# Two gather turns moved into the experts' program, batch 1's gathers moved up, and the last batch's steps rearranged

## The reference

```
layer 0:  q = layernorm(x);  x += tanh(g) * causal_attention(q, ctx, ctx)        16 heads of 32
          w, sel = top 8 of 32 experts of softmax(layernorm(x) @ gate_w)
          x += tanh(g') * sum over the 8 of  w * down(silu(gate(row)) * up(row))
layer 1:  q = rms_norm(layernorm(x) @ wq + bq); k = rms_norm(ctx @ wk + bk); v = ctx @ wv + bv
          x += tanh(g) * (softmax(q k^T / sqrt(32)) v @ wo + bo)
          out = x + tanh(g') * (layernorm(x) @ ternary(weight) + bias)
```

## Time and profile before

| what | us |
|---|---|
| median of 3 runs | 1456.93 (1450.17 to 1460.65) |
| the profiled execution | 1449.55 |
| its span | 1447.8 |
| PE busy in the span | 1290.1 (89%) |
| layer 0, up to its barrier | about 297 |
| experts, up to their barrier | 922.0 |
| layer 1, first scores to last step's end | about 968 to 1409 |

### The profile page before, as it was taken

One profiled execution on the slowest core, in us unless ns is written; L12 is line 12 of the kernel. 1 busy time (PEld: TensorE's weight loads), 2 busy tenths in 40 slices (PEclk: granted clock), 3 DMA queues, 4 the chain that ended last, 5 costly groups with the idle time before them and its releaser, 6 DMA issues. The chain is left out here.

```text
span 1447.8 us, 39176 instructions
## 1 busy us (share of the span) xinstructions
PE 1290.1 (89%) x11501; PEld 836.5 (58%) x11502; DVE 940.0 (65%) x2347; ACT 897.2 (62%) x1845; POOL 519.5 (36%) x537
## 2 busy tenths in 40 slices
PE   3999999559999999999999999756899999999984
PEld 3777777425556656665556666333565656656652
DVE  4699897655566655656555633164777888888863
ACT  4777776325566666666566666425667777777661
POOL 2036564664335333321000000655544555552000
PEclk9999999779999999999999999978999999999997
DMA  3036445499888676766766544856646646653000
GB/s 104 31 130 224 181 171 184 173 311 324 290 309 282 235 234 226 244 213 215 233 229 210 193 146 145 167 89 88 102 69 108 106 71 117 103 72 75 16 8 23
DMA packets 96136, 233.49 MB, mean 161 GB/s; under 512 B 11808, under 2 KB 11808, under 8 KB 91424
## 3 DMA queue, kind: packets, MB, share of 16 engines
q0 software_dynamic: 33712, 113.79, 31.5%
q1 hardware_dynamic: 62320, 118.34, 24.6%
HBM read 140.84 MB, written 91.24 MB: 160 GB/s over the span
## 5 line engine op out<-in xcount | busy, mean ns | idle before, releaser
L1614 PE MATMUL bank<-wh,xT 128*128 x1280 | 340.1, 328 | 6.3 <-DVE hp L1729 5.4
L709 POOL DMA_INDIRECT xs<-y_tiles,slot_ix x120 | 191.2, 1593 | 219.9 <-DMA y_tiles<-ysb 99.9
L1614 PE MATMUL bank<-wl,xT 128*128 x640 | 209.4, 327 | 0.0
L1719 DVE SCALAR_TENSOR_TENSOR hv<-bank,sg 128x192 f32<-128x192 f32 x160 | 57.0, 356 | 220.1 <-ACT sg L1673 174.6
L1688 ACT ACTIVATE ysb<-bank,xg 128x512 f32<-128x512 f32 x160 | 110.0, 687 | 117.5 <-PE bank L1638 117.5
L1614 PEld LDWEIGHTS bank<-wh,xT 128*128 128x128 f16 x1280 | 125.6, 98 | 83.6 <-issue 13.4
L1667 ACT ACTIVATE xT<-bank 128x1024 f16<-128x1024 f16 x160 | 162.7, 1017 | 15.3 <-PE bank L1602 15.3
L1638 PE MATMUL bank<-wh,hT 128*128 x480 | 155.8, 379 | 0.8 <-issue 0.5
L1849 PE MATMUL bank<-w_hi,halfT 128*128 128x512 f16 x384 | 127.1, 393 | 23.5 <-DVE accb L1966 22.1
L334 ACT ACTIVATE l_probs<-bank,l_bias 128x256 f32<-128x256 f32 x256 | 118.9, 473 | 39.0 <-DVE l_bias L368 38.6
L1508 POOL DMA_DIRECT2D raw<-in_experts_dram x30 | 16.8, 560 | 333.2 <-DVE wl L1745 325.4
(11 more groups left out here) (282 smaller groups left out, 3060.4 us busy)
## 6 DMA issues: line engine op xcount, KB each, us to landing
xg<-x_slots SPq DMA_DIRECT2D x160, 272.0 KB, 2.8
y_tiles<-ysb SPq DMA_DIRECT2D x160, 256.0 KB, 2.7
raw<-in_experts_dram POOLq DMA_DIRECT2D x30, 1280.0 KB, 7.3
x_slots<-blank SPq DMA_DIRECT2D x33, 272.0 KB, 4.0
xs<-in_x_dram SPq DMA_DIRECT2D x8, 512.0 KB, 6.4
cbuf<-in_ctx_dram SPq DMA_DIRECT2D x8, 512.0 KB, 4.4
stage<-in_mats_dram POOLq DMA_DIRECT2D x4, 1024.0 KB, 6.4
room<-in_ctx_dram SPq DMA_DIRECT2D x8, 512.0 KB, 5.7
```

The lines of the kernel that those rows point to most:

```text
L709: return nc.gpsimd.indirect_dma_start(to, None, self.y_tiles[0 : (MT + 1 - k) * P, :], ix, compute_op=ALU.add)
L1614: last = nc.tensor.matmul(bGU[t.place % 2][:, 0:GU], xT[:, t.place % 2, xo + c * P : xo + (c + 1) * P], wp[:, bass.ds(w, 1), c * GU : (c + ...
```

## The change

It has four parts. `LAST_ADDS` falls from 4 to 2: six turns of batch 0 in the experts' list, two in layer 1's. In `BEGIN1`, DVE does `xc` before `P2` and `xn`, `sx` before `P3`, ACT does `sx` before `k0`, `k1`, and POOL issues three gathers of batch 1 before `P1`. For the last batch, a table `LAST1` takes the place of `SIDE1`: batch 6's post part is placed earlier in its steps, and `a0`, `b0`, `c0`, `d0` of batch 7 itself (words with `=`) in steps 11 to 15. The ten sends of batch 6 that follow `pw` lose their waits.

```
-LAST_ADDS = 4
+LAST_ADDS = 2
 BEGIN1 = dict(
-    act=["sc", "T0", "T1", "P0", "P1", "k0", "k1", "sx", "T2", "T3", "P4", "P5", "k2", "k3"],
+    act=["sc", "T0", "T1", "P0", "P1", "sx", "k0", "k1", "T2", "T3", "P4", "P5", "k2", "k3"],
-    dve=["sc", "P0", "P1", "P2", "P3", "xc", "xn", "sx", "k0", "k1", "P4", "S0", "S1", "P5", ...
+    dve=["sc", "P0", "P1", "xc", "P2", "xn", "sx", "P3", "k0", "k1", "P4", "S0", "S1", "P5", ...
+LAST1 = dict(
+    pe={0: ["a0"], 1: ["a1"], 2: ["<c0"], 3: ["c1"], 4: ["<d0"], 5: ["<d1"], 8: ["<g0", "g1"], 9: ["h0"], 10: ["h1"], 11: ["=a0"],
+        13: ["<=c0"], 14: ["=d0"]},
+    act={1: ["b0", "b1"], 2: ["c0"], 3: ["c1"], 7: ["f0", "f1"], 8: ["g0"], 9: ["g1"], 12: ["=b0"], 13: ["=c0"]},
+    pool={5: ["d1"]},
+    dve={0: ["a0", "a1"], 1: ["b0"], 2: ["<b1"], 4: ["d0"], 5: ["d1"], 6: ["e"], 7: ["f0", "f1"], 10: ["h0"], 11: ["h1"],
+         12: ["<=a0", "=b0"], 15: ["=d0"]})
-def side1(table, b, step, early, do_prep, do_post):
+def side1(eng, b, step, early, do_prep, do_post):
+    table = LAST1[eng] if b.n == B - 1 else SIDE1[eng]
...
+        if piece.startswith("="):
+            do_post(b, piece[1:])
+        elif piece in ORDER_PREP1:
...
 (layer 0, POOL's end)
-            for n in (1, 2):
-                pool.wait_ge(xe_norm, QT * (B - 1) + n)
-                send_next()
-            for n in (1, 2):
-                pool.wait_ge(post_copied, 2 * (B - 1) + n)
-                send_next()
-            for n in (11, 12, 13, 14, 16, 18):
-                pool.wait_ge(dve_post, marks + n)
+            while sends[0] < SENDS * (B - 1):
                 send_next()
...
+        LAST_USES = ["a0", "c0", "d0", "a1", "c1", "d1", "g0", "g1", "h0", "h1"]
...
 (dve_post_, piece a)
+                if is_last(b):
+                    dve.wait_ge(at.probs_made, STEPS * b.n + STEPS // 2 * (t + 1))
+                    chain.link(v.reciprocal(rsum[:, t, :], at.sums[:, b.par, t, :]))
+                elif t == 0:
                     dve.wait_ge(at.probs_made, STEPS * b.n + STEPS)
                     chain.link(v.reciprocal(rsum[:, :, :], at.sums[:, b.par, :, :]))
...
-            before = {"P1": 0, "xc": 0, "P5": 6}
+            before = {"P1": 3, "xc": 0, "P5": 6}
```

More of the change, by code:

```diff
@@ L227, in last_pieces1 @@
 def last_pieces1(eng):
-    return [piece for piece in ORDER_POST1 if any(piece == word.lstrip("<") for words in SIDE1[eng].values() for word in words)]
+    done = [word.lstrip("<=") for words in LAST1[eng].values() for word in words if "=" in word]
+    return [piece for piece in ORDER_POST1 if any(piece == word.lstrip("<") for words in SIDE1[eng].values() for word in words) and piece not in done]
 class Attention:
@@ L1834, in layer1, with is_last, uses_of, reads_of @@
         USES = ["a0", "a1", "c0", "c1", "d0", "d1", "g0", "g1", "h0", "h1"]
+        LAST_USES = ["a0", "c0", "d0", "a1", "c1", "d1", "g0", "g1", "h0", "h1"]
         COPIED = ["c0", "c1", "g0", "g1"]
-        READ = [u for u in USES if u not in COPIED]
+        def is_last(b):
+            return isinstance(b.n, int) and b.n == B - 1
+        def uses_of(b):
+            return LAST_USES if is_last(b) else USES
+        def reads_of(b):
+            return [u for u in uses_of(b) if u not in COPIED]
         def mine(b, t):
@@ L1986, in pe_post @@
                 return
-            k, t = USES.index(piece), int(piece[1])
-            before = USES[k - 1]
+            k, t = uses_of(b).index(piece), int(piece[1])
+            before = uses_of(b)[k - 1]
             if before in COPIED:
@@ L1992, in pe_post @@
             else:
-                pe.wait_ge(po_read, 6 * b.n + 1 + (READ.index(before) + 1 if k else 0))
+                pe.wait_ge(po_read, 6 * b.n + 1 + (reads_of(b).index(before) + 1 if k else 0))
             if piece[0] == "a":
@@ L2040, in dve_post_ @@
             elif piece[0] == "d":
-                dve.wait_ge(po_ps, 10 * b.n + 5 + t)
+                dve.wait_ge(po_ps, 10 * b.n + uses_of(b).index(piece) + 1)
                 v.scalar_tensor_tensor(att[:, t, :], bPost[:, :], 1.0 / (SC_A * SC_W), vec[:, B_O, :], ALU.mult, ALU.add).then_inc(po_read, 1)
-                dve.wait_ge(po_read, 6 * b.n + 4 + t)
+                dve.wait_ge(po_read, 6 * b.n + reads_of(b).index(piece) + 2)
                 chain.link(v.scalar_tensor_tensor(mine(b, t), att[:, t, :], gates[:, 1:2], mine(b, t), ALU.mult, ALU.add))
@@ L2061, in dve_post_ @@
                 v.scalar_tensor_tensor(outb[:, t, :], outb[:, t, :], gates[:, 3:4], mine(b, t), ALU.mult, ALU.add).then_inc(out_ready, 1)
-                if t == QT - 1:
+                if t == QT - 1 and not is_last(b):
                     chain.end("post1")
@@ L2176, in body @@
                 for s in range(STEPS):
-                    side1(SIDE1["dve"], b, s, True, do_prep, do_post)
+                    side1("dve", b, s, True, do_prep, do_post)
                     at.dve_step(dve, b, s, more, before=b.n > 0)
-                    side1(SIDE1["dve"], b, s, False, do_prep, do_post)
+                    side1("dve", b, s, False, do_prep, do_post)
             over_batches(lambda b: body(b, True), lambda b: body(b, True), lambda b: body(b, False))
@@ L2201, in body @@
                 for s in range(STEPS):
-                    at.pe_step(pe, b, s, more, before=b.n > 0, between=lambda: side1(SIDE1["pe"], b, s, True, do_prep, do_post))
-                    side1(SIDE1["pe"], b, s, False, do_prep, do_post)
+                    at.pe_step(pe, b, s, more, before=b.n > 0, between=lambda: side1("pe", b, s, True, do_prep, do_post))
+                    side1("pe", b, s, False, do_prep, do_post)
             over_batches(lambda b: body(b, True), lambda b: body(b, True), lambda b: body(b, False))
```

13 lines of the change are left out of this document (6 added, 7 removed).

## The result

The kernel before takes 1456.93 us in the median of seven runs, the changed one 1443.31 (1437.92 to 1447.80): ratio **0.9912**, 95% interval 0.9884 to 0.9940, some 12.8 us less (the two medians are 13.6 apart). 1443 was forecast. A second comparison on another chip gave 0.9891 (0.9855 to 0.9928). The profiled execution took 1441.69 us with a span of 1439.9, so it is only 7.9 us ahead of the profiled one of before; where these 7.9 are can be read, and they are not the sum that was forecast.

What follows compares the result with a forecast made beforehand. Middle steps were taken as bound by PE, with PE idle awaiting batch 1's gathers and partly idle in the last batch. 10.1 + 2.4 + 1.2 = 13.7 us off 1456.9 gave 1443, range 1432 to 1452.

Steps and rivals of the forecast that it cites:

- 10.1 + 2.4 + 1.2: Forecast gains in us: batch 1's last gather landing earlier, the last batch of layer 1, layer 0's unpaced sends.
- each chain makes one per landing: Batch 1's gathers behind xc's power: one per 5.1 us landing in each chain; then intervals of 2.68 us to the sixteenth.
- So only the semaphore waits hold the barrier: Barrier behind the experts: waits for gathers to land, not POOL's engine, hold it; it opens some 3.2 us later.
- 3.8 + 1.3 + 1: Last batch's steps, us added: PE's extra pieces 3.8, short waits against old idle time 1.3, late `=d0` about 1.
- less 1.7 of low clock that follows the 4.15 stop no longer: Last batch's steps: removing the 4.15 us stop in front of `g0` saves 1.7 us of PE's low clock.
- fourth rival: Short waits in the last batch's steps drop PE to its low level for good: plus 19 us, 1476; chance 0.04.
- no wait in my list is over 1.8: Argument against PE's clock falling in the last batch's steps: the listed waits are at most 1.8 us.
- third rival: Last batch gains nothing or loses a few us, or gathers land late: 7 to 9 us gained, 1449; chance 0.15.
- The 9.7 us that the prediction priced it at: Layer 0's end: by the skill's rule at its worst, unpaced sends lose ten times 0.97 us; the sum becomes 4.0.

Runs made afterwards that it cites:

- e8: Changed kernel with one gather turn of batch 0 moved into the experts' part, not two; 0.9920 of the kernel before.
- e7: Changed kernel with unread matmuls filling PE's waits in and behind the last batch's steps; 0.9881 of the kernel before.
- e9: Changed kernel with the old last batch (SIDE1) and unread matmuls in front of PE's waits there; 0.9904 of the kernel before.
- e3: Changed kernel with the ten sends of layer 0's last batch waiting for their pieces of work as before; 0.9933 of the kernel before.
- e12: Kernel before with the unpaced sends alone; 1.0010 of the kernel before.
- e5: The changed kernel itself, run again on another chip; 0.9891 of the kernel before.
- e10: Kernel before with the new last batch alone; 0.9997 of the kernel before.
- e1: Changed kernel with layer 1's last batch as in the kernel before; 0.9925 of the kernel before.

## Why the prediction was right, and where it was wrong

**The time** was right: 13.7 us less were forecast, 12.8 measured. The sum behind it, 10.1 + 2.4 + 1.2, is less so, as the stretches show: 8.2, minus 1.5, and nothing that can be seen. A total that fits this well with terms that are off by 7 us together is in part luck.

**The start: mechanism right, size too large.** In the profiled pair the chain came out almost as written: first gather of layer 1 at 928.87 (928.8 plus 1.1 to 1.4 forecast), the second addition at 940.66 (940.5), the power at 945.33 (945.4), `P5` at 960.66 (960.4), the sixteenth gather at 977.95 (978.1), the statistics at 982.88 (983.1). But fourteen profiles show that this pair was a good one: from G to X1 90.49 us in the mean of four with the old start and 82.28 of nine with the new, 8.2 and not 10.1. Two terms were too large. The power comes 42.5 us behind G in the mean with the old start and 41.6 with the new, 0.9 earlier and not 2.0; the profile of before has 43.19, the longest of its four. And from the power to X1 7.3 us are gained and not 8.1 (48.0 against 40.7). The step at fault there is "each chain makes one per landing", with an interval of 2.68 us from one execution for all: from the tenth gather to the sixteenth the nine have 2.65 to 3.04, 2.87 in the mean.

**The barrier.** "So only the semaphore waits hold the barrier" is right (e8, and ACT's row at 926.08). The wait that holds it is the one named: turn 3's second gather starts at 919.55 and takes 6.3 us to land (`DMA to landing` of that row), so at 925.85, and POOL's queue is through at 925.9. The barrier moved by 3.98 us and not 3.2, since the prediction took the median of all gathers, 5.1, for this one; the trace of before has 6.5 for it. It cost nothing that can be seen, as forecast: POOL's next gather followed the last one within 1.96 us.

**The last batch: wrong by 3.9 us.** 2.4 us less were forecast; the mean of seven profiles with the new table is 107.7 from X7 to E (105.5 to 109.5), that of four with the old one 106.2 (105.6 to 107.6): 1.5 more. The gain of 2.4 is out by this; that it is a loss is not certain, as the two groups overlap. The part behind the steps is right within a microsecond: 6.0 shorter in the mean (13.97 against 19.95), 6.8 forecast. So are the added pieces and waits: 3.8 + 1.3 + 1, 6.1, against 6.3 measured with the clock held (e7, e9). The step that failed is **"less 1.7 of low clock that follows the 4.15 stop no longer"**. It took the low clock for a thing that a long stop brings and short stops don't. From the copy in step 0 to the one behind the last step the new table takes 48.5 in the mean and 45.95 filled: 2.5 us of low clock in the steps. The old one takes 41.0 and 39.63: 1.4. So the term is plus 1.1 and not minus 1.7, and the steps are 7.5 longer, not 4.4. The fourth rival had this mechanism, and had ruled it out by the size of the waits ("no wait in my list is over 1.8"): behind one of 1.85 the clock did fall. But it did not stay down, as the windows of the changed kernel's profile show, so its price was a few us, not 19. The third rival named the size.
```profile
1362.00:1364.00 2.00, 1.27 (x17) 0.95 (x18) 1.95 (x4) 1.98 (x6) 0.00 (x0) 0.97 0.00 0
1364.00:1366.00 2.00, 2.00 (x14) 1.45 (x12) 0.86 (x2) 1.92 (x6) 0.00 (x0) 0.50 0.00 0
1366.00:1368.00 2.00, 2.00 (x18) 1.47 (x14) 0.40 (x1) 0.70 (x1) 0.00 (x0) 0.68 0.00 0
1368.00:1372.00 4.00, 3.62 (x24) 1.81 (x25) 1.24 (x4) 2.64 (x10) 0.00 (x0) 1.00 0.02 4
```

**The sends.** 1.2 us, and nothing that can be measured came: 1.0010 alone. Behind layer 0's last power the changed kernel's last batch of sends began 14.4 us later and not 17.7, but its last one started after 39.4 and not 39.6 us. All fourteen profiles agree, and they show where the 3.3 us go: only the first four of these sends stand in layer 0, and the fifth, the first in the experts' program, starts 23.0 us behind the power with unpaced sends and 22.9 with paced ones (24.0 in e3). In the changed kernel POOL's engine is idle for 2.41 us in front of it. The prediction reckoned with the first send going some 4 us earlier; twelve of the sixteen stand behind layer 0's barrier and did not. The first tile came 25.6 to 26.2 us behind that power on PE in ten executions with unpaced sends, 26.9 to 29.7 in four with paced ones. By the tenth tile both kinds lay among each other (64.4 to 70.0 and 63.0 to 68.8): a head start of 1 to 4 us was lost in a scatter of 6. Nothing was lost either: eight of the ten sends took the same 0.97 us, the others 1.29 and 1.40. The Trainium skill's trap ("SBUF — State Buffer", "DVE blocks DMA"), by which GpSimd cannot write descriptors while certain DVE operations run, would have made the edit a loss. The 9.7 us that the prediction priced it at would be 1.0067 in e12 and are out.

**What stays open.** The stretches account for 6.7 us (8.2 less 1.5), and the three parts alone add up to 5.2 (0.0003, 0.0043 and minus 0.0010 of 1455), with an uncertainty of some 5. The whole was measured at 12.8 and, on the other chip, 16.6, each with an uncertainty of 4 to 6. Taking parts away from the whole gives, by the ratios against the first comparison's 0.9912, 2 us for the last batch, 7 for the start and 3 for the sends, and against e5's 0.9891 it gives 5, 11 and 6, each with an uncertainty of 6 to 7. For the last batch the times even point the other way than the stretches; its part alone (e10, 0.9997) lies between. Whether the parts help each other, or the scatter of a time that hangs on the clock made the difference, these runs cannot tell. Of the 13.7 us, then, about 7 are found in their places.

No version beats the changed kernel by a measurable amount: e7 is at 0.9881, 1.5 us ahead of it on the same chip with intervals that overlap widely, though its last batch is 5 us shorter than the mean of the others.

## What to carry to other kernels

Work that is moved out of a tail into steps that have idle time is only worth its length if the engine keeps its clock there: cost the new short waits also as clock, and try cheap matmuls in front of them before another order. A barrier behind POOL's gathers is held by the queues' waits, so look for the last wait and not for the last gather. Where a change's parts are worth 0.5% each, cut several profiled executions at the same marks before a term is believed: one pair of profiles said 10.0 for the start and minus 3.8 for the last batch, and the means of several said 8.2 and minus 1.5. And ask of every operation that is to go earlier on which side of a barrier it stands.

## What the runs showed of the hardware

The same stop brings the clock down in one execution and not in the next: behind 1.85 us without PE work in step 2, the window up to step 8 had a mean granted clock of 0.87 to 0.89 in four executions, 0.93 in two and 0.96 in one; and the old table, whose stop there is 1.66 us, had 1.00 in three and 0.91 in one. Filled, both had 1.00. While the clock is low the eight matmuls of an `h` take 3.59 us and not 1.90, and behind the last step, where PE waits between single pieces, some 2.6 us went to the clock (13.97 against 11.39).

On the chips of e1 to e8 layer 0 ran slower from its third batch on (41 us a batch, 30 in the six other profiles), and both kernels took some 70 us longer. The granted clock there is lower (0.88 from 140 to 180 us in e5, 1.00 in the changed kernel's profile), but it is not shown to be the cause: ACT and DVE together stand idle in these layers for 71 to 79 us in waits whose end the profile puts down to nothing on this core (`remote`), and the other six profiles have no such wait. What they are stays open. One from e5:
```profile
156.93 0.87 ACT L624 ACTIVATE l_probsT<-bank 128x384 f32<-128x384 f32 x2 [3.98 <-remote]
```
